# One exponential over two PSUM banks in a causal attention loop

## The chip, the cores and the metric

The kernel runs on all 8 NeuronCores of one Trainium2 chip, each core on its own sequence of 2048 tokens, with no traffic between cores. The metric is the device time of the slowest core in microseconds (us). The engines are named as in the profile: PE (TensorE, matmul), PEld (TensorE's weight load), DVE (VectorE), ACT (ScalarE), POOL (GpSimd) and SP (SyncE).

## The reference, cut to what matters

One pre-norm transformer layer: causal attention with 8 heads of width 128 over 2048 tokens, and then a mixture of experts with 8 experts and a shared one. The change is in the attention alone.

```python
x = x + attn(layernorm(x))
x = x + moe(layernorm(x))
# attn, for each batch entry b and head h
s = einsum('bihd,bjhd->bhij', q, k) / 128
s = s - 1e30 * (i < j)
p = softmax(s, axis=-1)
o = einsum('bhij,bjhd->bihd', p, v)
```

## The kernel before

The program writes out one instruction list for each engine. Every engine works through its list strictly in order and waits on semaphores. Each DVE, ACT and POOL instruction also waits for the one before it on its own engine. PSUM has eight banks of 128 x 512 F32, `ps[0]` to `ps[7]`. `bank_prod` emits a matmul that waits until the earlier readers of its bank are done (`bank.frees`), and `bank_cons` emits a reader that waits until the bank is written (`bank.ready`).

The work runs in this order: loading and transposing x, layernorm, then the heads, the output projection, a second layernorm, the router, and the nine experts. For each head h there are three stages in a row: `emit_passA(h)` (a bound on the scores, with squares on POOL), `emit_qkv_rope(h+1)` (projection and rotation for the next head) and `emit_passB(h)`, which holds the change.

`emit_passB` loops over four query chunks `qc` of 512 queries. A chunk has `nkt = 4*qc + 4` key tiles of 128 keys: 4, 8, 12 and 16, so 40 in a head and 320 on a core. For one key tile `kt` the steps are:

- S (L595): a matmul writes the scores, 128 keys x 512 queries, into bank 4 for an even `kt` and bank 5 for an odd one.
- mask (L601), for the last four key tiles of a chunk (the diagonal ones): DVE adds the mask to the bank in place.
- exp (L607): ACT writes exp(scores) as bf16 into one of the two halves of `pT`.
- O (L581) and L (L586): two matmuls that accumulate the output in bank 6 and the row sums in bank 7. They are always issued for the previous key tile, kept in `pend`.

So PE's list reads S0, S1, OL0, S2, OL1, S3, and so on: OL(k) stands behind S(k+1) and ahead of S(k+2). OL(k) waits for exp(k), and S(k+2) needs the bank that exp(k) read.

A chunk ends with the reciprocal of the row sums on DVE (L616), an F32 matmul that spreads it over the partitions through bank 5 (L620), its copy (L623) and the scaling of the output (L627). S0 of the next chunk follows L620 on PE at once. S1 waits for the copy L623, because it uses bank 5.

Of the kernel before, what the change touches and what calls it, by code (L numbers as in the profile page):

```python
# [7 lines left out]
F32 = mybir.dt.float32  # L8
BF16 = mybir.dt.bfloat16
AF = mybir.ActivationFunctionType  # L10
# [4 lines left out]
DM = 1024  # L15
NH = 8
DH = 128
# [100 lines left out]
def build_nc(dbg=False):  # L118
    nc = bass.Bass("TRN2", target_bir_lowering=False)
# [33 lines left out]
    big = nc.alloc_sbuf_tensor("big", [128, 32768], BF16)  # L153
# [1 line left out]
    csn = nc.alloc_sbuf_tensor("csn", [128, 4096], BF16)  # L155
    s_sb = nc.alloc_sbuf_tensor("s_sb", [128, 3072], F32)
    maskm = nc.alloc_sbuf_tensor("maskm", [128, 896], BF16)
    pT = nc.alloc_sbuf_tensor("pT", [128, 1024], BF16)
    identb = nc.alloc_sbuf_tensor("identb", [128, 128], BF16)
    identf = nc.alloc_sbuf_tensor("identf", [128, 128], F32)  # L160
    pmat_sb = nc.alloc_sbuf_tensor("pmat_sb", [128, 128], BF16)
    onesb = nc.alloc_sbuf_tensor("onesb", [128, 1], BF16)
    ones1 = nc.alloc_sbuf_tensor("ones1", [1, 128], F32)
    rwT = nc.alloc_sbuf_tensor("rwT", [128, KC * 8], BF16)
    rw_raw = nc.alloc_sbuf_tensor("rw_raw", [8, DM], BF16)
    bias_rep = nc.alloc_sbuf_tensor("bias_rep", [128, 8], F32)
    cwtok = nc.alloc_sbuf_tensor("cwtok", [128, 128], F32)
    lg_sb = nc.alloc_sbuf_tensor("lg_sb", [128, 128], F32)
# [14 lines left out]
    negmh = nc.alloc_sbuf_tensor("negmh", [128, 1], F32)  # L183
    mh_sb = nc.alloc_sbuf_tensor("mh_sb", [1, 8], F32)

    bigf = big[:, :].bitcast(F32)
    csnf = csn[:, :].bitcast(F32)
    sf = s_sb

    ps = [PsBank(nc.alloc_psum_tensor(f"ps{i}", [128, 512], F32).ap()) for i in range(8)]  # L190

    stack = ExitStack()
    mk = lambda name: Ch(stack.enter_context(nc.semaphore(name)))
# [15 lines left out]
    ac = mk("ac")  # L209
# [4 lines left out]
    b = Builder()  # L214
# [8 lines left out]
    def bank_prod(bank, fn, waits=(), last=True):  # L223
        w = list(waits) + bank.frees
        toks = b.emit("tensor", fn, waits=w, incs=[(pe, 1)] if last else ())
        bank.frees = []
        if last:
            bank.ready = toks[0]
            return toks[0]
        return None  # L230

    def bank_cons(bank, eng, fn, waits=(), ch=dv):
        w = list(waits) + ([bank.ready] if bank.ready else [])
        tok = b.emit(eng, fn, waits=w, incs=[(ch, 1)])[0]
        bank.frees.append(tok)
        return tok
# [3 lines left out]
    t_mask = dma(ld, "sync", maskm[:, :], d["c_mask"])  # L240
# [54 lines left out]
    for g4 in range(4):  # L295
# [5 lines left out]
        for ti in range(4):  # L301
            tt = g4 * 4 + ti
            for kc in range(KC):
# [5 lines left out]
                          waits=[tok_ld, t_identf])  # L309
                dstc = kc * T + tt * 128  # L310
                bank_cons(bank, "vector",
                          lambda e, o=x_sb[:, dstc:dstc + 128], i=pap: e.tensor_copy(o, i))
# [4 lines left out]
    for kc in range(KC):  # L317
# [4 lines left out]
                  waits=[t_rw, t_identb])  # L322
        bank_cons(bank, "vector",
                  lambda e, o=rwT[:, kc * 8:(kc + 1) * 8], i=pap: e.tensor_copy(o, i))
# [3 lines left out]
                                              start=True, stop=True),  # L328
              waits=[t_eb, t_ones1])
    bank_cons(bank, "vector",  # L330
              lambda e, o=bias_rep[:, :], i=pap: e.tensor_copy(o, i))
# [180 lines left out]
    rope_done = [None] * NH  # L512
# [51 lines left out]
    def emit_passB(h, t_negmh):  # L564
        par = h % 2
        half = h // 4
        hh = h % 4
        qs = q_slice(par)
        ks = k_slice(par)
        for qc in range(NTS):  # L570
            ob = ps[6]
            lb = ps[7]
            nkt = 4 * qc + 4
            pend = None

            def emit_ol(item, s1):
                tex_, vsl_, ptb_, kt_ = item
                bank_prod(ob,
                          lambda e, o=ob.ap[:, :], l=vsl_, r=ptb_,
                          s0=(kt_ == 0), s1_=s1:  # L580
                          e.matmul(o, l, r, start=s0, stop=s1_),  # L581
                          waits=[tex_, t_v_done[half]], last=s1)
                bank_prod(lb,
                          lambda e, o=lb.ap[0:1, :], r=ptb_,
                          s0=(kt_ == 0), s1_=s1:
                          e.matmul(o, onesb[:, :], r, start=s0, stop=s1_),  # L586
                          waits=[tex_], last=s1)

            for kt in range(nkt):
                sb_ = ps[4 + (kt % 2)]  # L590
                bank_prod(sb_,
                          lambda e, o=sb_.ap[:, :],
                          l=ks[:, kt * 128:(kt + 1) * 128],
                          r=qs[:, qc * 512:(qc + 1) * 512]:
                          e.matmul(o, l, r, start=True, stop=True),  # L595
                          waits=rope_done[h])
                if kt >= 4 * qc:
                    moff = 384 - 128 * (kt - 4 * qc)
                    tmk = bank_cons(sb_, "vector",
                                    lambda e, o=sb_.ap[:, :],  # L600
                                    m=maskm[:, moff:moff + 512]: e.tensor_add(o, o, m),  # L601
                                    waits=[t_mask])
                    sb_.ready = tmk
                ptb = pT[:, (kt % 2) * 512: (kt % 2) * 512 + 512]
                tex = bank_cons(sb_, "scalar",
                                lambda e, o=ptb, i=sb_.ap[:, :]:
                                e.activation(o, i, AF.Exp, bias=negmh[:, 0:1],  # L607
                                             scale=1.0 / DH),
                                waits=[t_negmh], ch=ac)
                vsl = big[:, kt * 512 + hh * 128: kt * 512 + hh * 128 + 128]  # L610
                if pend is not None:
                    emit_ol(pend, s1=False)
                pend = (tex, vsl, ptb, kt)
            emit_ol(pend, s1=True)
            til = bank_cons(lb, "vector",
                            lambda e, o=invl_row, i=lb.ap[0:1, :]: e.reciprocal(o, i))  # L616
            bank5 = ps[5]
            bank_prod(bank5,
                      lambda e, o=bank5.ap[:, :]:
                      e.matmul(o, ones1[:, :], invl_row, start=True, stop=True),  # L620
                      waits=[til])
            tsc = bank_cons(bank5, "vector",
                            lambda e, o=scale_rep, i=bank5.ap[:, :]: e.tensor_copy(o, i))  # L623
            ocol = o_col + h * T + qc * 512
            bank_cons(ob, "vector",
                      lambda e, o=big[:, ocol:ocol + 512], i=ob.ap[:, :]:
                      e.tensor_mul(o, i, scale_rep),  # L627
                      waits=[tsc])
        qk_free[par] = (pe, pe.n)
        pT_free[0] = (pe, pe.n)  # L630
# [3 lines left out]
    for h in range(NH):  # L634
        t_negmh = emit_passA(h)
# [14 lines left out]
    for mc in range(2):  # L650
        dwo = wo_slice(mc % 2).rearrange("p (c n) -> p c n", c=KC)
        t_wo_mc[mc] = dma(wd_wo[mc % 2], "gpsimd", dwo, wo_flat[:, :, mc * 128:(mc + 1) * 128],
                          waits=[qk_free[mc % 2]])
    for mc in range(KC):
        par = mc % 2
        for ts in range(NTS):
            bank = ps[(mc * NTS + ts) % 4]
            for c in range(KC):
                ocol2 = o_col + c * T + ts * 512
                bank_prod(bank,  # L660
                          lambda e, o=bank.ap[:, :],
                          l=wo_slice(par)[:, c * 128:(c + 1) * 128],
                          r=big[:, ocol2:ocol2 + 512],
                          s0=(c == 0), s1=(c == KC - 1):
                          e.matmul(o, l, r, start=s0, stop=s1),  # L665
                          waits=[t_wo_mc[mc], t_o_all], last=(c == KC - 1))
            xcol = mc * T + ts * 512
            bank_cons(bank, "vector",
                      lambda e, o=x_sb[:, xcol:xcol + 512], i=bank.ap[:, :]:
                      e.tensor_add(o, o, i),  # L670
                      waits=dbg_x0_tok)
        if mc + 2 < KC:
# [3 lines left out]
                                  waits=[(pe, pe.n)])  # L676
    t_x2 = (dv, dv.n)
    if dbg and "o" in dbg:
        dbg_gate_x2.append(dma(st, "sync", d["d_o"], big[:, 8192:24576],
                               waits=[t_o_all]))  # L680
# [7 lines left out]
    for tt in range(NTT):  # L688
        bank = ps[4 + tt % 2]
        for kc in range(KC):  # L690
            bank_prod(bank,
                      lambda e, o=bank.ap[:, 0:8],
                      l=xn_sb[:, kc * T + tt * 128: kc * T + (tt + 1) * 128],
                      r=rwT[:, kc * 8:(kc + 1) * 8],
                      s0=(kc == 0), s1=(kc == KC - 1):
                      e.matmul(o, l, r, start=s0, stop=s1),
                      waits=[xn_tok[tt // 4]], last=(kc == KC - 1))
        t_lg.append(bank_cons(bank, "vector",
                              lambda e, i=bank.ap[:, 0:8],
                              o=lg_sb[:, tt * 8:(tt + 1) * 8]:  # L700
# [7 lines left out]
    def m1bc(t):  # L708
# [3 lines left out]
           waits=t_lg, incs=[(dv, 1)])  # L712
# [3 lines left out]
           incs=[(dv, 1)])  # L716
    vnop()
    b.emit("vector", lambda e: e.tensor_max(m1a[:, :], kd128[:, 0:32:2], kd128[:, 1:32:2]),
           incs=[(dv, 1)])
    vnop()  # L720
    b.emit("vector", lambda e: e.tensor_sub(kd128[:, :], lg_sb[:, :], m1bc(m1a)),
           incs=[(dv, 1)])
# [3 lines left out]
           incs=[(dv, 1)])  # L726
    vnop()
    b.emit("vector", lambda e: e.tensor_scalar_mul(mska[:, :], km1a[:, :], -3e38),
           incs=[(dv, 1)])
    vnop()  # L730
    b.emit("vector", lambda e: e.tensor_add(mska[:, :], lg_sb[:, :], mska[:, :]),
           incs=[(dv, 1)])
# [3 lines left out]
           incs=[(dv, 1)])  # L736
# [3 lines left out]
           incs=[(dv, 1)])  # L740
    vnop()
    b.emit("vector", lambda e: e.tensor_max(m2a[:, :], kd128[:, 0:32:2], kd128[:, 1:32:2]),
           incs=[(dv, 1)])
    vnop()
    b.emit("vector", lambda e: e.tensor_sub(d12a[:, :], m1a[:, :], m2a[:, :]),
           incs=[(dv, 1)])
    vnop()
    b.emit("vector", lambda e: e.tensor_sub(kd128[:, :], lg_sb[:, :], m1bc(m2a)),
           incs=[(dv, 1)])
# [3 lines left out]
                 incs=[(dv, 1)])[0]  # L753
    tp1 = b.emit("scalar", lambda e: e.activation(p1a[:, :], d12a[:, :], AF.Sigmoid),
                 waits=[t_d], incs=[(ac, 1)])[0]
    tp2 = b.emit("scalar", lambda e: e.activation(p2a[:, :], d12a[:, :], AF.Sigmoid,
                                                  scale=-1.0),
                 incs=[(ac, 1)])[0]
# [3 lines left out]
           waits=[tp1], incs=[(dv, 1)])  # L762
# [3 lines left out]
           waits=[tp2], incs=[(dv, 1)])  # L766
    vnop()
    tcw = b.emit("vector", lambda e: e.tensor_add(cwtok[:, :], mska[:, :], kd128[:, :]),
                 incs=[(dv, 1)])[0]
    for tt in range(NTT):  # L770
# [3 lines left out]
                  lambda e, o=papt, i=cwtok[:, tt * 8:(tt + 1) * 8]:  # L774
                  e.transpose(o, i, identf[:, :]),
                  waits=[tcw])
        t_cw_rows.append(
            bank_cons(bankt, "vector",
                      lambda e, o=csnf[0:8, tt * 128:(tt + 1) * 128], i=papt:
# [4 lines left out]
    if dbg and "cw" in dbg:  # L784
        t_cw_rows = t_cw_rows + [dma(st, "sync", d["d_cw"], cwtok[:, :],
                                     waits=t_cw_rows)]
    if dbg and "lg" in dbg:
        t_cw_rows = t_cw_rows + [dma(st, "sync", d["d_lg"], lg_sb[:, :],
                                     waits=t_cw_rows)]
# [43 lines left out]
    for ei, e_ in enumerate(e_order):  # L833
# [3 lines left out]
        if not shared:  # L837
# [3 lines left out]
            else:  # L841
                tok_cp = dma(sw_cw, "sync", csnf[0:1, 0:2048], csnf[e_:e_ + 1, 0:2048],
                             waits=[(pe, pe.n)] + t_cw_rows)
                cwsrc = csnf[0:1, 0:2048]
                tok_cwsrc = [tok_cp]
            for tsb in range(NTS):
                bank = ps[tsb % 2]
                bank_prod(bank,
                          lambda e, o=bank.ap[:, :],
                          r=cwsrc[0:1, tsb * 512:(tsb + 1) * 512]:  # L850
# [180 lines left out]
```

How the kernel before makes its waits and increments, by code:

```python
        def run(e, ws=ws, fn=fn, rincs=rincs):  # L75
            for sem, v in ws:
                e.wait_ge(sem, v)
            inst = fn(e)
            for sem, amt in rincs:
                inst = inst.then_inc(sem, amt)
```

## Time and profile before

| | us |
|---|---|
| median of 3 runs (4823.49 to 4825.1) | 4824.67 |
| the profiled execution, its own time | 4822.22 |
| its span on the slowest core (core 2) | 4820.7 |
| spans of the eight cores | 4816.1 to 4820.7 |
| PE busy | 4021.4 (83%) |
| DVE busy | 1557.8 (32%) |
| ACT busy | 581.5 (12%) |
| the 320 exps of L607 | 219.9 in all, 0.687 each |

The profile is of one execution. Times in rows of the timeline are counted from the start of the span. A matmul row begins when the matmul starts; matmuls are pipelined and their ends are modelled, so the distance from start to start says what one costs. In square brackets a row has the idle time of its engine before it and what ended that. The mean granted TensorE clock over the span is 0.885 of full speed on every core; in single stretches it is either 0.50 (1.2 GHz) or 1.00 (2.4 GHz).

### The profile page before, as it was taken

To read this page: it belongs to the slowest core of one execution; us is meant where nothing else is said; L and a number is where in the kernel's file an instruction comes from. 1 tells how busy PE (TensorE), PEld (TensorE's weight loads), DVE (VectorE), ACT (ScalarE), POOL (GpSimd) and SP (SyncE) were. 2 spreads that over 40 slices of the span, in tenths; PEclk is the share of its full clock that TensorE was granted. 3 is DMA by queue.
4 is the path that set the end of the run, shared out by engine and by line. 5 is a ranking of instruction groups with operands and counts; after the bars stand their busy time and mean duration, and the time that the engine had idled before them with its cause. 6 is when DMAs were issued, how large, how long until landed. Compare 5 with 4: busy or idle time off the path is not lost.

```text
span 4820.7 us, 48101 instructions; the slowest of 8 cores (4816.1 to 4820.7 us)
## 1 busy us (share of the span) xinstructions
PE 4021.4 (83%) x16329; PEld 1672.1 (35%) x16650; DVE 1557.8 (32%) x2516; ACT 581.5 (12%) x933; POOL 668.8 (14%) x649
## 2 busy tenths in 40 slices
PE   5365566555574699999999999999999999999998
PEld 2021112111121244444444444444444444444443
DVE  4633333333336332232232232332322322322324
ACT  0002220112220010010010110110110110110100
POOL 0621101111104311011111110110110110111100
PEclk9576677676686699999999999999999999999996
DMA  4000000000010243343343334334333433434422
GB/s 99 0 9 5 5 5 5 5 0 5 3 11 5 27 40 37 34 40 37 35 40 38 36 37 39 35 36 40 35 37 35 40 36 36 40 35 40 39 28 79
DMA packets 480750, 143.01 MB, mean 30 GB/s; under 512 B 473738, under 2 KB 476154, under 8 KB 480514
## 3 DMA queue, kind: packets, MB, share of 16 engines
q0 software_dynamic: 475488, 122.72, 26.4%
q1 hardware_dynamic: 5026, 17.20, 1.0%
q8 instruction: 141, 2.31, 0.2%
q14 instruction: 95, 0.78, 0.1%
HBM read 254.15 MB, written 8.39 MB: 54 GB/s over the span
## 4 chain that ended last, share of the span: by engine, by line
PE 79%; DVE 11%; issue 4%; POOL 3%; ACT 2%; DMA 1%; DVEq 0%; ACTq 0%; POOLq 0%; SPq 0%
PE ps L871 21%; PE ps L932 21%; PE ps L884 20%; PE ps L480 3%; DVE s_sb L616 2%; PE ps L581 2%; PE ps L586 2%; PE ps L595 2%; PE ps L620 1%; DVE xn_sb L351 1%; ACT pT L607 1%; POOL pT L528 1%; PE ps L665 1%; PE ps L456 1%; POOL big L508 1%
## 5 line engine op out<-in xcount | busy, mean ns | idle before, releaser
L871 PE MATMUL ps<-xn_sb,w_sb 128*128 128x512 bf16 x4515 | 1054.3, 384 | 10.0 <-DVE s_sb L855 4.9
L884 PE MATMUL ps<-xn_sb,w_sb 128*128 128x512 bf16 x4515 | 1034.9, 379 | 4.9
L932 PE MATMUL ps<-big,w_sb 128*128 128x512 bf16 x4516 | 1003.9, 382 | 30.1 <-DVE big L906 25.1
L901 DVE TENSOR_TENSOR s_sb<-ps,s_sb 128x512 bf16<-128x512 f32 x512 | 354.2, 692 | 1178.5 <-PE ps L884 1102.8
L220 POOL DMA_DIRECT2D w_sb<-w x360 | 333.9, 931 | 2777.2 <-PE ps L884 1800.6
L892 ACT ACTIVATE s_sb<-ps 128x512 bf16<-128x512 f32 x576 | 344.0, 597 | 2636.6 <-PE ps L871 2422.5
L932 PEld LDWEIGHTS ps<-big,w_sb 128*128 128x128 bf16 x4608 | 454.1, 99 | 580.0 <-issue 46.6
L871 PEld LDWEIGHTS ps<-xn_sb,w_sb 128*128 128x128 bf16 x4608 | 454.7, 99 | 573.8 <-issue 43.0
L884 PEld LDWEIGHTS ps<-xn_sb,w_sb 128*128 128x128 bf16 x4608 | 450.9, 98 | 543.7
L941 DVE TENSOR_TENSOR x_sb<-x_sb,ps 128x512 f32<-128x512 f32 x288 | 198.0, 687 | 836.8 <-PE ps L932 792.1
L607 ACT ACTIVATE pT<-ps,negmh 128x512 bf16<-128x512 f32 x320 | 219.9, 687 | 682.8 <-DVE ps L601 414.4
L906 DVE TENSOR_TENSOR big<-s_sb 128x512 bf16<-128x512 bf16 x576 | 245.2, 426 | 63.0 <-DVE s_sb L901 3.7
L581 PE MATMUL ps<-pT,big 128*128 128x512 bf16 x315 | 144.3, 458 | 75.4 <-ACT pT L607 62.6
L601 DVE TENSOR_TENSOR ps<-ps,maskm 128x512 f32<-128x512 f32 x128 | 89.6, 700 | 278.1 <-PE ps L595 275.1
L595 PE MATMUL ps<-big 128*128 128x512 bf16 x307 | 147.5, 481 | 24.4 <-DVE s_sb L623 14.4
L620 PE MATMUL ps<-s_sb,ones 1*128 1x512 f32 x64 | 65.3, 1121 | 117.3 <-DVE s_sb L616 117.3
L528 POOL TENSOR_TENSOR pT<-big 128x512 bf16<-128x512 bf16 x64 | 66.4, 1038 | 596.7 <-PE ps L620 546.7
L586 PE MATMUL ps<-pT,onesb 128*1 128x512 bf16 x320 | 141.4, 442 | 4.9 <-DVE ps L601 3.5
L480 PE MATMUL ps<-xn_sb,w_sb 128*128 128x512 bf16 x498 | 139.1, 444 | 3.6 <-DVE big L460 1.6
L495 PE MATMUL ps<-s_sb,pmat_sb 128*128 128x512 bf16 x64 | 31.8, 497 | 122.3 <-DVE s_sb L491 122.3
L616 DVE RECIPROCAL s_sb<-ps 1x512 f32<-1x512 f32 x32 | 107.0, 3345 | 62.0 <-PE ps L586 62.0
L508 POOL TENSOR_TENSOR big<-s_sb 128x512 bf16<-128x512 f32 x64 | 80.7, 1261 | 293.1 <-DVE s_sb L504 293.1
(108 smaller groups left out, 1503.2 us busy)
## 6 DMA issues: line engine op xcount, KB each, us to landing
w_sb<-w POOLq DMA_DIRECT2D x288, 256.0 KB, 5.1
w_sb<-w POOLq DMA_DIRECT2D x72, 512.0 KB, 6.8
big<-x SPq DMA_DIRECT2D x4, 2048.0 KB, 15.7
out<-big SPq DMA_DIRECT2D x4, 2048.0 KB, 6.6
w_sb<-wv POOLq DMA_DIRECT2D x2, 1024.0 KB, 21.1
w_sb<-wq POOLq DMA_DIRECT2D x8, 256.0 KB, 6.0
w_sb<-wk POOLq DMA_DIRECT2D x8, 256.0 KB, 6.7
w_sb<-wo POOLq DMA_DIRECT2D x8, 256.0 KB, 4.5
```

What stands on the lines that cost most here:

```text
L220: return b.emit(eng, lambda e, o=out_ap, i=in_ap: e.dma_start(out=o, in_=i), waits=waits, incs=[(ch, 16)], nochain=True)[0]
L480: e.matmul(o, l, r, start=s0, stop=s1),
L581: e.matmul(o, l, r, start=s0, stop=s1_),
L586: e.matmul(o, onesb[:, :], r, start=s0, stop=s1_),
L595: e.matmul(o, l, r, start=True, stop=True),
L607: e.activation(o, i, AF.Exp, bias=negmh[:, 0:1], scale=1.0 / DH),
L871: e.matmul(o, l, r, start=s0, stop=s1),
L884: e.matmul(o, l, r, start=s0, stop=s1),
L892: lambda e, o=sb_b, i=gb_.ap[:, :]: e.activation(o, i, AF.Silu),
L901: e.tensor_mul(o, i, c),
L906: e.tensor_mul(o, a, bb),
L932: e.matmul(o, l, r, start=s0, stop=s1),
```

## The change

The key tiles are taken in pairs. Both S matmuls of a pair are issued, both masks where there are masks, and then one exp over banks 4 and 5 together: 128 x 1024 instead of two of 128 x 512. For that the eight PSUM banks become slices of one allocation, and `pT` doubles to two halves of 1024 columns. Both O/L pairs of matmuls wait for the one exp. `pend` still holds back one key tile, so the loop at the end of the pair issues OL of the odd tile of the previous pair and then OL of the even tile of this pair. PE's list now reads S0, S1, OL0, S2, S3, OL1, OL2, S4, S5, OL3, OL4, and so on.

`rw_raw`, the landing place of the router weights, moves from an own buffer into `big`, beyond the part in which x is staged. Its DMA stays where it was in POOL's list.

```diff
-    pT = nc.alloc_sbuf_tensor("pT", [128, 1024], BF16)
+    pT = nc.alloc_sbuf_tensor("pT", [128, 2048], BF16)
-    rw_raw = nc.alloc_sbuf_tensor("rw_raw", [8, DM], BF16)
+    rw_raw = big[0:8, 16384:16384 + DM]
-    ps = [PsBank(nc.alloc_psum_tensor(f"ps{i}", [128, 512], F32).ap()) for i in range(8)]
+    PS = nc.alloc_psum_tensor("psall", [128, 4096], F32)
+    ps = [PsBank(PS[:, i * 512:(i + 1) * 512]) for i in range(8)]
+    ps45 = PS[:, 2048:3072]
...
-            for kt in range(nkt):
-                sb_ = ps[4 + (kt % 2)]
-                bank_prod(sb_,
...
-                ptb = pT[:, (kt % 2) * 512: (kt % 2) * 512 + 512]
-                tex = bank_cons(sb_, "scalar",
-                                lambda e, o=ptb, i=sb_.ap[:, :]:
-                                e.activation(o, i, AF.Exp, bias=negmh[:, 0:1],
-                                             scale=1.0 / DH),
-                                waits=[t_negmh], ch=ac)
-                vsl = big[:, kt * 512 + hh * 128: kt * 512 + hh * 128 + 128]
-                if pend is not None:
-                    emit_ol(pend, s1=False)
-                pend = (tex, vsl, ptb, kt)
+            for kp in range(nkt // 2):
+                for ki in range(2):
+                    kt = 2 * kp + ki
+                    sb_ = ps[4 + ki]
+                    bank_prod(sb_,
...
+                ptb2 = pT[:, (kp % 2) * 1024: (kp % 2) * 1024 + 1024]
+                w = [t_negmh, ps[4].ready, ps[5].ready] + ps[4].frees + ps[5].frees
+                tex = b.emit("scalar",
+                             lambda e, o=ptb2: e.activation(o, ps45, AF.Exp,
+                                                            bias=negmh[:, 0:1],
+                                                            scale=1.0 / DH),
+                             waits=w, incs=[(ac, 1)])[0]
+                ps[4].frees.append(tex)
+                ps[5].frees.append(tex)
+                for ki in range(2):
+                    kt = 2 * kp + ki
+                    vsl = big[:, kt * 512 + hh * 128: kt * 512 + hh * 128 + 128]
+                    ptb = pT[:, (kp % 2) * 1024 + ki * 512: (kp % 2) * 1024 + ki * 512 + 512]
+                    if pend is not None:
+                        emit_ol(pend, s1=False)
+                    pend = (tex, vsl, ptb, kt)
```

## Rows read from the trace of the kernel before

**Rows 1.** The page, busy us (share of the span) and count of instructions.

```profile
PE 4021.4 (83%) x16329; PEld 1672.1 (35%) x16650; DVE 1557.8 (32%) x2516; ACT 581.5 (12%) x933; POOL 668.8 (14%) x649
```

**Rows 2.** Groups by line and shape on ACT: busy us, mean ns | idle before.

```profile
L892 ACT ACTIVATE s_sb<-ps 128x512 bf16<-128x512 f32 x576 | 344.0, 597 | 2636.6 <-PE ps L871 2422.5 <-remote 182.6 <-ACT s_sb L892 6.7
L607 ACT ACTIVATE pT<-ps,negmh 128x512 bf16<-128x512 f32 x320 | 219.9, 687 | 682.8 <-DVE ps L601 414.4 <-PE ps L595 230.1 <-PE ps L620 36.1
L389 ACT ACTIVATE s_sb<-s_sb 1x512 f32<-1x512 f32 x8 | 5.0, 628 | 269.6 <-DVE s_sb L387 269.6
...
L549 ACT ACTIVATE mh_sb<-mh_sb 1x1 f32<-1x1 f32 x8 | 1.6, 202 | 0.7
```

**Rows 3.** Timeline, head 2, third chunk: a diagonal pair, then the chunk's end.

```profile
686.45 0.39 PE L595 MATMUL ps<-big 128*128 128x512 bf16 x1
...
687.01 0.70 DVE L601 TENSOR_TENSOR ps<-ps,maskm 128x512 f32<-128x512 f32 x1 [8.47 <-PE ps L595]
...
687.86 0.69 ACT L607 ACTIVATE pT<-ps,negmh 128x512 bf16<-128x512 f32 x1 [1.24 <-DVE ps L601]
...
689.31 0.39 PE L595 MATMUL ps<-big 128*128 128x512 bf16 x1
...
692.49 0.38 PE L581 MATMUL ps<-pT,big 128*128 128x512 bf16 x1 [0.25 <-ACT pT L607]
...
693.35 3.35 DVE L616 RECIPROCAL s_sb<-ps 1x512 f32<-1x512 f32 x1 [1.84 <-PE ps L586]
```

**Rows 4.** Timeline, the same chunk: a pair without mask at full clock.

```profile
682.47 0.39 PE L595 MATMUL ps<-big 128*128 128x512 bf16 x1
...
683.01 0.69 ACT L607 ACTIVATE pT<-ps,negmh 128x512 bf16<-128x512 f32 x1 [0.37 <-PE ps L595]
...
683.84 0.38 PE L581 MATMUL ps<-pT,big 128*128 128x512 bf16 x1
...
684.46 0.39 PE L595 MATMUL ps<-big 128*128 128x512 bf16 x1
```

**Rows 5.** Timeline, the second chunk: a pair without mask at half clock.

```profile
660.59 0.61 PE L595 MATMUL ps<-big 128*128 128x512 bf16 x1
...
663.55 0.61 PE L595 MATMUL ps<-big 128*128 128x512 bf16 x1
```

**Rows 6.** Timeline, the third chunk's first pair, at half clock.

```profile
676.81 0.61 PE L595 MATMUL ps<-big 128*128 128x512 bf16 x1
...
677.89 0.59 PE L595 MATMUL ps<-big 128*128 128x512 bf16 x1 [0.47 <-DVE s_sb L623]
...
678.63 0.69 ACT L607 ACTIVATE pT<-ps,negmh 128x512 bf16<-128x512 f32 x1 [0.37 <-PE ps L595]
...
679.72 0.61 PE L595 MATMUL ps<-big 128*128 128x512 bf16 x1
```

**Rows 7.** Timeline, the first chunk: masks of its first pair, its second pair, its end.

```profile
644.30 1.50 DVE L601 TENSOR_TENSOR ps<-ps,maskm 128x512 f32<-128x512 f32 x2
...
647.00 0.61 PE L595 MATMUL ps<-big 128*128 128x512 bf16 x1
...
647.79 0.70 DVE L601 TENSOR_TENSOR ps<-ps,maskm 128x512 f32<-128x512 f32 x1 [1.99 <-PE ps L595]
...
650.95 0.58 PE L581 MATMUL ps<-pT,big 128*128 128x512 bf16 x1 [0.38 <-ACT pT L607]
...
652.22 3.35 DVE L616 RECIPROCAL s_sb<-ps 1x512 f32<-1x512 f32 x1 [2.25 <-PE ps L586]
```

**Rows 8.** Busy us (x) by stretch, head 2's third and fourth chunk; PEclk is the granted clock.

```profile
676.80:682.10 5.30, 4.62 (x10) 0.79 (x9) 1.38 (x2) 2.21 (x4) 0.00 (x0) 0.50 0.00 0
682.10:693.40 11.30, 8.87 (x28) 2.41 (x27) 2.85 (x5) 6.04 (x9) 0.00 (x0) 1.00 0.00 0
698.80:706.00 7.20, 5.98 (x13) 1.14 (x13) 1.38 (x2) 3.31 (x5) 0.00 (x0) 0.50 0.00 0
706.00:720.10 14.10, 11.29 (x36) 3.15 (x35) 2.86 (x5) 7.68 (x12) 0.00 (x0) 1.00 0.01 1
```

More of the change, by code:

```diff
@@ L587, in emit_ol @@
                           waits=[tex_], last=s1)
-            for kt in range(nkt):
-                sb_ = ps[4 + (kt % 2)]
-                bank_prod(sb_,
[L592 to L603, printed above, removed]
-                ptb = pT[:, (kt % 2) * 512: (kt % 2) * 512 + 512]
-                tex = bank_cons(sb_, "scalar",
-                                lambda e, o=ptb, i=sb_.ap[:, :]:
-                                e.activation(o, i, AF.Exp, bias=negmh[:, 0:1],
-                                             scale=1.0 / DH),
-                                waits=[t_negmh], ch=ac)
-                vsl = big[:, kt * 512 + hh * 128: kt * 512 + hh * 128 + 128]
-                if pend is not None:
-                    emit_ol(pend, s1=False)
-                pend = (tex, vsl, ptb, kt)
@@ new lines, in emit_passB @@
+            for kp in range(nkt // 2):
[3 more added lines that the diff above has]
+                    bank_prod(sb_,
+                              lambda e, o=sb_.ap[:, :],
+                              l=ks[:, kt * 128:(kt + 1) * 128],
+                              r=qs[:, qc * 512:(qc + 1) * 512]:
+                              e.matmul(o, l, r, start=True, stop=True),
+                              waits=rope_done[h])
+                    if kt >= 4 * qc:
+                        moff = 384 - 128 * (kt - 4 * qc)
+                        tmk = bank_cons(sb_, "vector",
+                                        lambda e, o=sb_.ap[:, :],
+                                        m=maskm[:, moff:moff + 512]: e.tensor_add(o, o, m),
+                                        waits=[t_mask])
+                        sb_.ready = tmk
+                ptb2 = pT[:, (kp % 2) * 1024: (kp % 2) * 1024 + 1024]
[14 more added lines that the diff above has]
+                    pend = (tex, vsl, ptb, kt)
```

## The prediction

> **What bounds the kernel now.** The page comes first: PE is busy for 83% of the span and ACT for 12% [rows 1]. That average is mostly the experts, which the change does not touch. So the groups by line on ACT come next. They say what the removed thing is worth where it stands: the 320 exps take 219.9 us, but ACT stood idle for 682.8 us ahead of them, 414.4 of it until a mask and 230.1 until a score matmul [rows 2]. ACT is starved in this stage, so its busy time is not what sets the stage's length. What does is read from the timeline of one head's pass B, in four pieces, together with the granted clock by stretch.
>
> In what follows a pair is the way from the S matmul of an even key tile to the S matmul of the next even tile. Before the change it is a closed chain, because S(k+2) stands behind OL(k) on PE and OL(k) waits for exp(k).
>
> - Without mask, at full clock, the chain is S start to exp start 0.54, exp 0.69, exp end to O start 0.14, and O and L together 0.62 until the next S. The sum is 1.99, and the two S starts are 1.99 apart [rows 4]. PE could issue the six matmuls in 6 x 0.31 = 1.86, so PE and the chain are nearly level.
> - Without mask at half clock PE itself is the bound: 2.96 for six matmuls, 0.49 each [rows 5].
> - Diagonal, at full clock, the mask comes in: S start to mask start 0.56, mask 0.70, 0.15, exp 0.69, 0.14, O and L 0.62. That is 2.86, and the S starts are 2.86 apart [rows 3].
>
> **The change part by part.** The order on PE matters most. Before, OL(k) had S(k+1) and OL(k-1) between it and its own S. In the new list the pair's exp can start only after both S matmuls (and both masks), and ahead of the waiting OL(2p) stands only OL(2p-1), two matmuls. Behind the waiting instruction on PE are L(2p) and both S matmuls of the next pair, and behind those on DVE and ACT the next masks and the next exp. So the longer exp, the second S and the second mask all enter the chain in series. Nothing covers them.
>
> *The length of the new exp, E.* No row shows a 1024-column one. From below: 128 x 512 without the pointer to a bias takes 597 ns and 1 x 1 takes 202, so 0.773 ns for each further element, and E is at least 687 + 512 x 0.773 = 1083 ns. The same step from 1 x 1 to 1 x 512 in one kind of operand gives (628 - 202) / 511 = 0.834, and E = 687 + 427 = 1114 ns. From above, two exps: 2 x 687 = 1374 ns, if crossing into the second bank cost a new start [rows 2]. I take 1.11 us, because the second pair of rows varies only the number of elements. The Trainium skill, page "ScalarE: Activation LUTs", section "What ACT_TABLE_LOAD costs", gives about 280 ns + 0.833 ns per element with a bias held in a pointer operand. By it the exp would be 1133 ns, and the sum below 160 x 0.02 = 3 us more.
>
> Each kind of pair is now chained again, with the same gaps:
>
> - *No mask, full clock:* second S 0.31 after the first (PE's pitch, half of the 0.62), then 0.54, 1.11, 0.14, 0.62 = 2.72 against 1.99 [rows 4]. That is +0.73.
> - *No mask, half clock:* second S 0.49 later, S to exp 0.74 [rows 6], 1.11, 0.14, O and L 2 x 0.49 = 3.46 against 2.96 [rows 5]. That is +0.50.
> - *First pair of a chunk, except in the first chunk:* S1 waits for L623 and starts 1.08 after S0; then 0.74, 1.11, 0.14, 0.98 = 4.05 against 2.91 [rows 6]. That is +1.14.
> - *Diagonal pair, full clock:* the second mask starts 0.80 after the first, since two of them take 1.50 with 0.70 each [rows 7]. Then 0.56 + 0.80 + 0.70 + 0.15 + 1.11 + 0.14 + 0.62 = 4.08 against 2.86 [rows 3]. That is +1.22.
> - *Last pair of a chunk, from its S to the reciprocal, full clock:* before, 693.35 - 689.31 = 4.04. After: 3.46 until the first O, 0.62 to the second O and 0.86 from there to the reciprocal = 4.94 [rows 3]. That is +0.90.
> - *The first chunk, at half clock:* its first pair before takes 2.70 from the first mask to the next S (647.00 - 644.30); after, 0.80 + 0.70 + 0.15 + 1.11 + 0.14 + 0.98 = 3.88, so +1.18. Its last pair before takes 5.22; after, 0.79 + 0.80 + 0.70 + 0.15 + 1.11 + 0.14 = 3.69 to the first O, 0.98 to the second, 1.27 to the reciprocal = 5.94, so +0.72 [rows 7].
>
> *Counting.* A head has 20 pairs: in the first chunk 2; in the others one first pair, 1, 3 and 5 middle pairs without mask, one diagonal and one last pair. The clock decides which price the middle ones have. In head 2 it is at 0.50 for the first 5.3 us of the third chunk and the first 7.2 us of the fourth, and at 1.00 for the rest, through diagonal stretches with gaps as well [rows 8]. That is the first pair and about one middle pair in each chunk at half clock. I keep that by pairs: 3 middle ones at half clock, 6 at full. A head then costs 1.18 + 0.72 + 3 x 1.14 + 3 x 0.50 + 6 x 0.73 + 3 x 1.22 + 3 x 0.90 = 17.6 us. Eight heads: 141 us.
>
> *The rest costs nothing.* The 160 exps saved shorten ACT's busy time by 160 x (1.374 - 1.114) = 42 us, but ACT waits here anyway, and after the change PE waits for a longer one instead. The PSUM slices are the same banks. `rw_raw` moves to columns that nothing else writes before the router weights are transposed; the DMA keeps its place, and its cover is the load of x. The larger `pT` adds no instruction. The stages around pass B depend on its last matmul and its last scaling only, so they start later by the same amount. The weight loads for the next head, issued on POOL at the start of pass B, only get more time. Should one of these cost something after all, it is a single transfer or a start of a few us, not 320 times something.
>
> The sum against the profiled execution is 4822.2 + 141 = 4963. The median is 2.5 us above that execution, so the forecast for it is 4966 us, 2.9% slower.
>
> **The rivals.**
>
> *The clock stays at half (13 in 100).* The new chain leaves gaps in PE's work in every pair: at half clock 2.96 of 3.46 us are matmuls, at full clock 1.86 of 2.72, and in diagonal pairs 1.86 of 4.08. If the clock then never rises in pass B, a head pays more on 6 middle pairs (3.46 - 2.72 = 0.74), 3 diagonal ones (0.79 + 0.80 + 0.70 + 0.15 + 1.11 + 0.14 + 0.98 = 4.67, against 4.08: 0.59) and 3 last ones (5.94 - 4.94 = 1.00): 9.2 us. The time becomes 4966 + 74 = 5040. For it speaks that the clock falls to 0.50 behind each chunk's reciprocal already. Against it speaks that the clock held 1.00 through diagonal stretches in which PE idled for about a third [rows 3, 8]. The Trainium skill, page "TensorE: Matmul & The Clock Gate", section "A second HAM failure mode: psum-queue depth-cycling", reports that small PE pauses between groups of matmuls, made by cycling through PSUM banks, let the clock swing between the levels. The rows just named do not show such a swing inside a chunk, only at its end.
>
> *The clock rises at the same time, not at the same pair.* As the pairs are longer, less of the list would lie before the rise. That takes about 0.6 us from each of three chunks, 14 us in all: 4952. I count it with the forecast.
>
> *Crossing the bank costs a start (10 in 100).* With E = 1.374 every one of the 160 pairs is 0.26 longer: 4966 + 42 = 5008.
>
> *The clock falls in part (8 in 100).* If it drops in the long waits of diagonal pairs alone, up to 3 x (0.59 + 1.00) x 8 = 38 us are added: up to 5004.
>
> *The waits are hidden (5 in 100, within 0.2%).* This would be so if both OLs of the previous pair stood behind the new S matmuls: four matmuls, 1.24 us, would then lie beside the exp. It needs an order on PE other than the one the list has; PE does no later matmul before one that waits.
>
> *ACT is what counts (2 in 100, faster).* If the stage were as long as ACT's list, the saving of 0.26 us for each pair would come back: 4825 - 42 = 4783. It decides only where ACT is busy back to back, which needs ACT's idle 682.8 us near nothing [rows 2]. To be faster by the chain, a pair without mask would need E under 1.99 - 0.31 - 0.54 - 0.14 - 0.62 = 0.38 us, less than the exp of 512 columns takes.
>
> **How the numbers follow.** The forecast case holds 62 in 100, with its own range of 4940 to 4985. Below, it is the 4952 of the earlier rise, 5 us less for E = 1.083, and 7 us for a second S that starts a little sooner than the 0.31 of an average matmul. Above, it is one more middle pair at half clock in three chunks of each head, 3 x 0.74 x 8 = 18 us. The range of 4935 to 5020 takes in the long exp and the part-time fall of the clock, and leaves out the clock that stays at half and the cases of no loss: 80 in 100. About 0.2% (10 us) is what a measurement of this kernel can tell from no change. Slower holds 0.93 (all cases but the last two), the same 0.04 and faster 0.03 (of the hidden waits 4 and 1 in 100, and the 2 of ACT).
>
> **What would show it right or wrong.** L607 should have 160 instructions of 128 x 1024 with a mean near 1114 ns; near 1374 would be the bank rival. PE's idle time ahead of L581, put down to L607, should be far longer than before. At full clock S matmuls of even tiles should be 2.7 us apart without mask and 4.1 with. From its first S to its reciprocal the third chunk should take 4.05 + 3.46 + 2 x 2.72 + 4.08 + 4.94 = 22.0 us, where it takes 16.5 now [rows 3, 6]. The stages outside pass B should keep their lengths. The prediction is wrong if PE's list in the trace shows four matmuls between the second S and the O that waits, or if the clock's rise comes much later than 5 to 7 us into a chunk.

## The result and the profile after

| | before | after |
|---|---|---|
| median, us | 4824.89 | 5031.92 |
| ratio | | 1.0443 (95% interval 1.041 to 1.0475) |
| profiled execution, us | 4822.22 | 5031.98 |
| span of the slowest core | 4820.7 | 5030.2 |
| mean granted TensorE clock | 0.885 | 0.842 |

The change costs 207 us. The forecast had the sign and the longer chain, but only 141 us; 5032 lies outside the range of 4935 to 5020. It lies next to the first rival (the clock stays at half, 5040), which had 13 in 100. In some executions the cores of one die run at a lower clock and take longer; the ratios here are those of executions without this, and for defer_pair and two_exps_late, whose medians it moves, the time given is the ratio times 4825.

Lines of the page of the changed kernel: the busy times, the granted clock in 40 slices, and two groups of pass B. Behind them stand the clock's line and the group of the O matmuls from the page of the kernel before.

```profile
PE 4118.9 (82%) x16329; PEld 1672.6 (33%) x16650; DVE 1557.5 (31%) x2516; ACT 539.6 (11%) x773; POOL 668.8 (13%) x649
...
PEclk9575556555555769999999999999999999999997
...
L583 PE MATMUL psall<-pT,big 128*128 128x512 bf16 x314 | 186.8, 595 | 179.8 <-ACT pT L611 179.8
L611 ACT ACTIVATE pT<-psall,negmh 128x1024 bf16<-128x1024 f32 x160 | 178.1, 1113 | 926.0 <-DVE psall L605 521.7
```

```profile
PEclk9576677676686699999999999999999999999996
...
L581 PE MATMUL ps<-pT,big 128*128 128x512 bf16 x315 | 144.3, 458 | 75.4 <-ACT pT L607 62.6
```

ACT has less to do, 539.6 us for 581.5 [rows 1], and is idle longer ahead of its exps, 926.0 us for 682.8 [rows 2]. An exp of 1024 columns takes 1113 ns. PE now waits 179.8 us for exps ahead of the O matmuls (L583), where it waited 62.6 us. In the clock's line (tenths of full speed, so half clock is 5), slices 4 to 13, where the heads run, show 5 and once 6; before, they showed 6 to 8.

The timeline of head 2, from the end of its first chunk through its second. "x2" is the two S matmuls of a pair, or its two masks.

```profile
707.26 3.35 DVE L626 RECIPROCAL s_sb<-psall 1x512 f32<-1x512 f32 x1 [3.73 <-PE psall L588]
...
712.72 0.61 PE L599 MATMUL psall<-big 128*128 128x512 bf16 x1
...
716.93 1.03 PE L599 MATMUL psall<-big 128*128 128x512 bf16 x2
...
718.12 1.11 ACT L611 ACTIVATE pT<-psall,negmh 128x1024 bf16<-128x1024 f32 x1 [2.46 <-PE psall L599]
...
719.38 0.58 PE L583 MATMUL psall<-pT,big 128*128 128x512 bf16 x1 [0.47 <-ACT pT L611]
...
720.41 1.03 PE L599 MATMUL psall<-big 128*128 128x512 bf16 x2
...
721.19 1.50 DVE L605 TENSOR_TENSOR psall<-psall,maskm 128x512 f32<-128x512 f32 x2 [6.74 <-PE psall L599]
...
722.84 1.11 ACT L611 ACTIVATE pT<-psall,negmh 128x1024 bf16<-128x1024 f32 x1 [3.61 <-DVE psall L605]
...
725.13 1.03 PE L599 MATMUL psall<-big 128*128 128x512 bf16 x2
...
728.83 0.59 PE L583 MATMUL psall<-pT,big 128*128 128x512 bf16 x1 [1.72 <-ACT pT L611]
...
731.16 3.35 DVE L626 RECIPROCAL s_sb<-psall 1x512 f32<-1x512 f32 x1 [3.74 <-PE psall L588]
```

The chain is the one that was forecast, link by link, at half clock: first pair 716.93 - 712.72 = 4.21 (forecast 4.05), pair without mask 3.48 (3.46), diagonal pair 725.13 - 720.41 = 4.72 (4.67), last pair 6.03 (5.94). What was not forecast is that the clock stays at half through the second and third chunk and almost to the end of the fourth. The busy times by stretch for this head's second, third and fourth chunk (the granted clock is the third number from the end):

```profile
712.70:731.20 18.50, 11.86 (x24) 2.20 (x24) 4.23 (x7) 4.45 (x4) 0.00 (x0) 0.50 0.01 1
736.60:762.00 25.40, 18.39 (x37) 3.29 (x36) 4.18 (x6) 6.68 (x6) 0.00 (x0) 0.50 0.00 0
767.50:799.00 31.50, 22.96 (x48) 4.32 (x48) 4.23 (x7) 8.91 (x8) 0.00 (x0) 0.55 0.00 0
```

Before, the same head's third and fourth chunk were at 1.00 after 5.3 and 7.2 us [rows 8].

The 32 reciprocals of a core give the length of every chunk: from one start to the next, less the 5.46 us between a reciprocal and the next chunk's first S (712.72 - 707.26). Means over the eight heads of the slowest core, in us, with the forecast sums beside them:

| chunk | before | forecast | half clock throughout | after |
|---|---|---|---|---|
| second | 13.0 | 4.05 + 3.46 + 4.08 + 4.94 = 16.5 | 18.1 | 18.2 |
| third | 16.9 | 22.0 | 4.05 + 3 x 3.46 + 4.67 + 5.94 = 25.0 | 25.2 |
| fourth | 21.0 | 27.4 | 32.0 | 32.1 |

The loss lies in pass B. On the slowest core the second to fourth chunks take 197 us more in all. The ways from a head's last reciprocal to the next head's first, with the first chunks in them, take 15 us more (forecast 8 x 1.90). From the last reciprocal to the end of the span it is 3421.1 us before and 3418.4 after.

### The profile page after: what moved, and what is told of

Same layout as the page of the kernel before. It is cut to its first block, busy times and chain, and to the rows that moved or that the text cites. A ratio compares the mean times of both kernels' runs of the same rounds, so it can differ in the third digit from the quotient of the medians.

```text
span 5030.2 us, 47621 instructions; the slowest of 8 cores (5019.8 to 5030.2 us)
## 1 busy us (share of the span) xinstructions
PE 4118.9 (82%) x16329; PEld 1672.6 (33%) x16650; DVE 1557.5 (31%) x2516; ACT 539.6 (11%) x773; POOL 668.8 (13%) x649
## 4 chain that ended last, share of the span: by engine, by line
PE 76%; DVE 11%; issue 4%; ACT 4%; POOL 3%; DMA 1%; DVEq 0%; ACTq 0%; POOLq 0%; another core or an unknown queue 0%; SPq 0%
PE psall L881 20%; PE psall L942 20%; PE psall L894 20%; ACT pT L611 4%; PE psall L482 2%; PE psall L599 2%; DVE s_sb L626 2%; PE psall L583 2%; PE psall L588 2%; DVE psall L605 2%; PE psall L630 1%; DVE xn_sb L353 1%; POOL pT L530 1%; PE psall L458 1%; PE psall L675 1%
## 5 line engine op out<-in xcount | busy, mean ns | idle before, releaser
L881 PE MATMUL psall<-xn_sb,w_sb 128*128 128x512 bf16 x4515 | 1051.6, 383 | 9.8 <-DVE s_sb L865 4.9
L894 PE MATMUL psall<-xn_sb,w_sb 128*128 128x512 bf16 x4515 | 1035.0, 379 | 4.8
L942 PE MATMUL psall<-big,w_sb 128*128 128x512 bf16 x4516 | 1003.1, 383 | 30.1 <-DVE big L916 25.2
L911 DVE TENSOR_TENSOR s_sb<-psall,s_sb 128x512 bf16<-128x512 f32 x512 | 354.2, 692 | 1175.4 <-PE psall L894 1100.2
L942 PEld LDWEIGHTS psall<-big,w_sb 128*128 128x128 bf16 x4608 | 453.6, 98 | 579.6 <-issue 45.2
L881 PEld LDWEIGHTS psall<-xn_sb,w_sb 128*128 128x128 bf16 x4608 | 453.6, 99 | 571.9 <-issue 39.2
L894 PEld LDWEIGHTS psall<-xn_sb,w_sb 128*128 128x128 bf16 x4608 | 450.4, 98 | 544.1
L902 ACT ACTIVATE s_sb<-psall 128x512 bf16<-128x512 f32 x576 | 343.9, 597 | 2635.5 <-PE psall L881 2421.6
L951 DVE TENSOR_TENSOR x_sb<-x_sb,psall 128x512 f32<-128x512 f32 x288 | 197.9, 687 | 836.0 <-PE psall L942 791.2
L583 PE MATMUL psall<-pT,big 128*128 128x512 bf16 x314 | 186.8, 595 | 179.8 <-ACT pT L611 179.8
L611 ACT ACTIVATE pT<-psall,negmh 128x1024 bf16<-128x1024 f32 x160 | 178.1, 1113 | 926.0 <-DVE psall L605 521.7
L588 PE MATMUL psall<-pT,onesb 128*1 128x512 bf16 x320 | 182.9, 571 | 11.7 <-ACT pT L611 11.4
L583 PEld LDWEIGHTS psall<-pT,big 128*128 128x128 bf16 x320 | 38.9, 122 | 312.0 <-issue 311.5
L482 PE MATMUL psall<-xn_sb,w_sb 128*128 128x512 bf16 x498 | 137.8, 441 | 3.6 <-DVE big L462 1.6
```

Of the source, the lines that this page charges most:

```text
L611: lambda e, o=ptb2: e.activation(o, ps45, AF.Exp, bias=negmh[:, 0:1], scale=1.0 / DH),
L902: lambda e, o=sb_b, i=gb_.ap[:, :]: e.activation(o, i, AF.Silu),
L911: e.tensor_mul(o, i, c),
```

## The experiments

All ran on 8 cores. Theories: A, the one exp waits for two scores and two masks with a single OL beside it, and the gaps this makes on PE also keep the clock down. B, the order on PE. C, the clock is low for a reason other than the gaps. D, the two-bank exp itself.

### two_exps: the order without the merge

```diff
-                tex = b.emit("scalar",
...
+                texs = []
+                for ki in range(2):
+                    sb_ = ps[4 + ki]
+                    ptb = pT[:, (kp % 2) * 1024 + ki * 512: (kp % 2) * 1024 + ki * 512 + 512]
+                    texs.append(bank_cons(sb_, "scalar",
...
-                    pend = (tex, vsl, ptb, kt)
+                    pend = (texs[ki], vsl, ptb, kt)
```

> The changed kernel with its order of matmuls on PE (S, S, OL of the odd tile before, OL of the even tile), but with two exps of 512 columns, and each O and L waiting for its own exp only. Theory A (the loss starts with the wait for one exp that needs both score matmuls and both masks): the chain of a pair is then again S to exp 0.54, 0.69, 0.14, O and L 0.62, so 1.99 us without mask and 2.86 with, as in the kernel before, and the time is 4825 us within 10, the mean clock 0.885. Rival B (the order on PE with a single OL as cover is the loss): 4950 us or more, clock about 0.845.

Measured: 4810.6 us, ratio 0.9969 (0.9958 to 0.9981), clock 0.885. B falls: the new order on PE costs nothing. It is even 15 us faster than the kernel before, more than the 10 us that I had allowed for. From its timeline, the last pair of head 2's first chunk and of its third:

```profile
643.57 1.03 PE L599 MATMUL psall<-big 128*128 128x512 bf16 x2
...
648.36 3.35 DVE L626 RECIPROCAL s_sb<-psall 1x512 f32<-1x512 f32 x1 [2.50 <-PE psall L588]
...
681.58 0.60 PE L599 MATMUL psall<-big 128*128 128x512 bf16 x2
...
684.44 0.60 PE L599 MATMUL psall<-big 128*128 128x512 bf16 x2
...
688.35 3.35 DVE L626 RECIPROCAL s_sb<-psall 1x512 f32<-1x512 f32 x1 [1.84 <-PE psall L588]
```

A diagonal pair takes 2.86, as before [rows 3]. The last pair takes 3.91 at full clock and 4.79 at half, against 4.04 [rows 3] and 5.22 [rows 7]. Its second S no longer stands behind an O that waits, so its mask and exp come earlier. That is 0.43 + 3 x 0.13 = 0.8 us a head, some 7 of the 15 us. Where the rest comes from was not looked for.

### two_exps_late: the wait without the merge

```diff
-                    pend = (texs[ki], vsl, ptb, kt)   # two_exps
+                    pend = (texs[1], vsl, ptb, kt)    # two_exps_late
```

> Two exps of 512 columns as in two_exps, but both OLs of a pair wait for the second one: the wait of the merged exp without the merge. The second exp ends 1.94 us after the first S at full clock where the merged one ends at 1.96, and at half clock the O starts 2.08 after the first S where the merged one lets it start at 2.48, so that PE has a gap of 0.12 instead of 0.5. Theory A: the wait itself costs 0.7 us a pair without mask at full clock, 0.8 a diagonal pair, 11.6 us a head, and the clock rises since the gaps at half clock are small: 4918 us within 25. Rival D (the two-bank exp is needed for the loss): 4811 us like two_exps.

Measured: ratio 1.0224 (1.0199 to 1.0248), 4933 us. The forecast was 4918 within 25. One changed wait costs 4933 - 4811 = 122 us, with exps of 512 columns as before; some of it comes through the clock, which is 0.874 to 0.879 where two_exps has 0.883 to 0.885. D falls as the main cause: the wait alone makes more than half of the loss.

### fill_all, fill_plain and fill_masked: the gaps and the clock

```diff
                     if pend is not None:
                         emit_ol(pend, s1=False)
+                    if ki == 0:
+                        filler(3 if kp >= 2 * qc else 1)   # fill_all
+                        filler(0 if kp >= 2 * qc else 1)   # fill_plain
+                        filler(3 if kp >= 2 * qc else 0)   # fill_masked
```

Each kernel is the changed one with one of the three lines; `filler(n)` issues n matmuls of 512 columns into bank 3, which nobody reads. The extra matmuls only add work.

> The changed kernel with extra matmuls of 512 columns into bank 3, which nobody reads, placed on PE right ahead of the O that waits for the exp: one in each pair without mask, three in each diagonal pair. At half clock the gap there is 0.47 us without mask and 1.72 with, and an extra matmul takes 0.49, so the chain itself gets at most 0.02 us longer in a pair. Theory A (the gaps that the merged exp leaves in each pair keep the granted clock at 0.50, and this is the difference between the 4966 forecast and the 5032 measured): the clock rises inside the chunks again, mean clock 0.88 or more, and the time falls to 4966 us within 20 in spite of the added work. Rival C (the clock is low for another reason, for instance the power drawn or the two-bank access): the clock stays at 0.84 and the time at 5032 to 5045 us.

Measured: 4954.73 us, ratio 1.0267 (1.0242 to 1.0292), clock 0.885. 288 extra matmuls make the changed kernel 77 us faster. Its third chunk in one head, in busy times by stretch and then in the timeline after the clock has risen:

```profile
715.10:720.10 5.00, 3.43 (x8) 0.71 (x8) 1.38 (x2) 1.11 (x1) 0.00 (x0) 0.50 0.00 0
720.10:737.00 16.90, 12.38 (x40) 3.01 (x38) 2.82 (x5) 5.57 (x5) 0.00 (x0) 0.93 0.00 1
```

```profile
722.66 0.60 PE L607 MATMUL psall<-big 128*128 128x512 bf16 x2
...
723.41 1.11 ACT L619 ACTIVATE pT<-psall,negmh 128x1024 bf16<-128x1024 f32 x1 [1.77 <-PE psall L607]
...
724.67 0.38 PE L583 MATMUL psall<-pT,big 128*128 128x512 bf16 x1 [0.57 <-ACT pT L619]
...
725.29 0.60 PE L607 MATMUL psall<-big 128*128 128x512 bf16 x2
...
727.92 0.61 PE L607 MATMUL psall<-big 128*128 128x512 bf16 x2
...
731.40 0.38 PE L583 MATMUL psall<-pT,big 128*128 128x512 bf16 x1 [1.60 <-ACT pT L619]
...
732.01 0.61 PE L607 MATMUL psall<-big 128*128 128x512 bf16 x2
...
736.98 3.35 DVE L636 RECIPROCAL s_sb<-psall 1x512 f32<-1x512 f32 x1 [2.89 <-PE psall L588]
```

Now the full-clock prices of the forecast can be read too: without mask 725.29 - 722.66 = 2.63 (forecast 2.72), diagonal 4.09 (4.08), last pair 4.97 (4.94). The chunks take 16.9, 22.2 and 27.3 us in the mean, against 16.5, 22.0 and 27.4 in the forecast. So with a clock that rises inside the chunks, as was assumed, the forecast of 4966 is met within 11 us. C falls. One thing stays open: the extra matmuls close the gaps and add work at the same time, and no run adds work without closing gaps.

> As the run with extra matmuls, but only the one in each pair without mask; the diagonal pairs keep their gaps. If the gaps of the pairs without mask decide the rise and a risen clock holds through the diagonal ones, the time is within 15 us of the run with all of them (4966 to 4980). If the diagonal gaps keep the clock down too, it lies near the middle, about 5000 us. If the gaps are not the cause, 5032 or more.

Measured: 4977.63 us, ratio 1.0316 (1.0296 to 1.0336), clock 0.870. Filling the pairs without mask takes off 54 of the 77 us. The time lies in the band of 4966 to 4980, but 23 us from fill_all and not within 15, so the diagonal gaps have a part: its second chunks, with one middle pair, still take 17.9 us in the mean.

> The complement of fill_plain: three extra matmuls in each diagonal pair of the changed kernel and none in the pairs without mask. fill_all took 77 us off and fill_plain 54. If the two kinds of gap act each in its own stretch, this one takes off the rest, 23 us: 5009 within 15, with a mean clock near 0.855. If the gaps of the pairs without mask alone decide, 5025 or more; if any filling is enough to raise the clock for a whole chunk, 4980 or less.

Measured: 4983.19 us, clock 0.868 to 0.876. The ratio is 1.0276 with a wide interval (1.018 to 1.0372), because the kernel before varied from 4824 to 4885 us beside it, so the time itself is used here. The expectation of 5009 was wrong, and 4983 is next to the 4980 of "any filling is enough": filling the diagonal pairs alone takes off 49 us, so the savings of the two kinds do not add up. The mean lengths of the second, third and fourth chunk are 16.9, 23.8 and 29.2 us here, 17.9, 22.6 and 28.3 in fill_plain and 16.9, 22.2 and 27.3 in fill_all: the diagonal gaps decide in the short second chunk, the others in the long ones. Busy times by stretch in one head: the third chunk in two parts, and the fourth.

```profile
721.30:738.70 17.40, 13.99 (x29) 2.65 (x29) 2.78 (x4) 4.75 (x5) 0.00 (x0) 0.50 0.00 0
738.70:745.50 6.80, 4.66 (x15) 1.03 (x13) 1.44 (x3) 1.94 (x2) 0.00 (x0) 0.89 0.01 2
750.90:777.80 26.90, 17.50 (x55) 4.31 (x54) 4.20 (x7) 8.91 (x8) 0.00 (x0) 0.88 0.00 0
```

In the third chunk the clock stays at half through the four pairs without mask and rises among the filled diagonal ones, as theory A has it. But in the fourth it rises within the unfilled pairs, at 757.1, 6 us into the chunk. This happens in four of eight heads, 6 to 10 us into the chunk (by the reciprocals, those four chunks take 26.9 to 27.7 us); in the other four it rises only among the filled diagonal pairs (30.9 to 31.5 us). The changed kernel has the same gaps there and stayed at half almost throughout; in head 2 it rose at 796, inside the last diagonal pair with its gap unfilled. So the gaps make the rise unlikely rather than forbid it; what decides it in a single chunk is open.

### defer_pair and four_banks_merged: covering the merged exp

```diff
+                for pp in pendl:
+                    emit_ol(pp, s1=False)
+                pendl = []
...
-                    if pend is not None:
-                        emit_ol(pend, s1=False)
-                    pend = (tex, vsl, ptb, kt)
+                    pendl.append((tex, vsl, ptb, kt))
...
+                bb = 4 if kp % 2 == 0 else 2    # four_banks_merged only
...
-                    sb_ = ps[4 + ki]
+                    sb_ = ps[bb + ki]           # four_banks_merged only
```

In four_banks_merged the exp reads the same two banks, `bb` and `bb + 1`.

> The changed kernel with its merged exp, but both OLs of a pair held back until after both S of the next pair, so that four matmuls lie beside the exp. Theory A: at half clock PE is fully busy without mask again (2.96 us a pair), so the clock rises as before; at full clock the next S waits for the exp, 0.31 + 0.54 + 1.11 + 0.14 = 2.10 against 1.99, a diagonal pair takes 3.46 against 2.86, the last pair of a chunk still 0.9 more. In all 6.6 us a head, so 4877 us within 20, clock 0.87 or more. Rival D (what costs is the two-bank exp itself, whatever is beside it): 5000 us or more.

Measured: ratio 1.0118 (1.0094 to 1.0142), 4882 us, clock 0.876 to 0.880. Two pairs of one chunk at full clock:

```profile
706.99 0.69 PE L600 MATMUL psall<-big 128*128 128x512 bf16 x2
...
709.09 0.59 PE L600 MATMUL psall<-big 128*128 128x512 bf16 x2 [0.26 <-ACT pT L612]
...
712.55 0.59 PE L600 MATMUL psall<-big 128*128 128x512 bf16 x2 [1.72 <-ACT pT L612]
```

2.10 and 3.46 us, exactly the chains that were worked out. With four matmuls beside the same exp, 150 of the 207 us are gone. In these rows PE still waits for the exp ahead of the next S, which needs the exp's banks.

> The merged exp with the OLs held back by a pair as in defer_pair, and the pairs' scores alternating between banks 4/5 and 2/3 (unused in pass B), so that the next S waits for no exp. Theory A: with the chain cut, PE is the bound without mask (1.86 us at full clock), the first pairs of the chunks overlap (0.8 us saved in each), the diagonal end is level with before: 4790 us within 25, the clock at 0.885. If instead the merged exp has a cost of its own, it stays above 4825.

Measured: 4800.13 us, ratio 0.9962 (0.9933 to 0.999), clock 0.887. With that chain cut, the merged exp stands in a kernel that is faster than the one before, by 25 us. D is out: the exp over two banks is no loss by itself.

### across_merged and across_single: a version that beats both

The chunks run into each other. The accumulators alternate, and the end of a chunk is issued in the next one.

```diff
+        acc = [(ps[6], ps[7]), (ps[0], ps[1])]
...
+            for pp in pendl:
+                emit_ol(pp)        # reciprocal right after a chunk's last OL
...
+            if qc > 0 and kp == 2:
+                finish(qc - 1)     # spreading matmul, copy, scaling
```

> As four_banks_merged, and the chunks run into each other: output and row sums alternate between banks 6/7 and 0/1, the reciprocal is taken at a chunk's end, and its spreading matmul and the scaling are issued after the third pair of the next chunk. The wait of 5.5 us for the reciprocal leaves PE's list in three of four chunks of a head, and the clock no longer falls there. Theory A: some 25 us a head less than before, 4600 to 4680 us, clock above 0.9. If DVE's 3.35 us reciprocal ahead of masks is in the way: nearer 4750.

Measured: 4605.69 us, ratio 0.9546 (0.9527 to 0.9565), clock 0.904. This is within what was expected.

> The same as across_merged with two exps of 512 columns, each O and L waiting for its own. It says whether the merged exp is worth something once nothing waits in its chain. Without mask both are bound by PE, so level there; with mask the first O of a pair can start 1.2 us earlier. I expect it 5 to 30 us faster than across_merged. If the fixed part of each exp counted, it would be slower.

Measured: 4567.9 us, ratio 0.9467 (0.9449 to 0.9486), clock 0.907. Two exps of 512 columns beat the merged one by 38 us, more than the 5 to 30 expected. The O matmuls in the span from 300 to 1650 us, first in across_merged, then in across_single, and the busy times of one head's pass B in across_single:

```profile
L584 PE MATMUL psall<-pT,big 128*128 128x512 bf16 x314 | 132.6, 422 | 45.1 <-ACT pT L634 44.5
...
L584 PE MATMUL psall<-pT,big 128*128 128x512 bf16 x314 | 124.5, 396 | 18.8 <-ACT pT L636 14.3
```

```profile
368.00:411.00 43.00, 39.14 (x123) 10.26 (x125) 25.55 (x27) 27.48 (x40) 3.00 (x3) 0.95 0.14 13
```

From a head's first reciprocal to its last it takes 37.0 us where the kernel before took 67.3, in the mean of eight heads, and the clock holds near full through pass B. ACT is busy for 27.48 of the 43 us. So even here the fixed part of each exp, which the merge saves, is not what counts. PE waits 30 us less for exps ahead of the O matmuls than in across_merged, which fits an O that can start on its own, earlier exp; where the other 8 us come from is open.

## Why the prediction was wrong

1. *ACT is starved, so fewer exps save nothing.* Right: ACT's busy time fell by 42 us and its wait ahead of the exps rose.
2. *E = 1.11 us.* Right: 1113 ns. The second bank costs no new start; 1374 is out, and with it that rival. The formula of the Trainium skill, page "ScalarE: Activation LUTs", section "What ACT_TABLE_LOAD costs", gives 1133: its 0.833 ns per element agrees with (1113 - 687) / 512 = 0.832 here, and its fixed part is 20 ns more than measured.
3. *The second S, the second mask and the longer exp enter the chain in series.* Right, at both clocks: 3.48, 4.72 and 6.03 at half; 2.63, 4.09 and 4.97 at full in fill_all. Only the 2.72 without mask was 0.09 too long: from the first S to the exp it is 723.41 - 722.66 = 0.75 at full clock, where 0.31 + 0.54 = 0.85 was taken. two_exps_late shows that the wait alone makes more than half of the loss, and defer_pair that cover takes most of it away.
4. *Counting: "I keep that by pairs: 3 middle ones at half clock, 6 at full."* This step failed. The clock's rise was carried over from a list in which PE had no gap in the pairs at half clock [rows 5] to one with 0.47 us in each and 1.72 us in each diagonal one. The rows that spoke against the rival showed the clock holding at 1.00 through gaps [rows 3, 8]; they did not show it rising through them. In place of the assumed rise, head 2 was at 0.50 through its second and third chunk, and at 0.55 in the mean of its fourth. With the pairs priced right, 9.2 us a head moved from the rival to the result: 4966 + 74 = 5040 for no rise at all, and 5032 measured, with a few rises among the eight heads. fill_all, which brings the rise back by other means, is 77 us faster than the changed kernel.
5. *The price of the rival was right, its chance was too low.* 13 in 100 rested on rows that could not exclude it, as step 4 says. The Trainium skill, page "TensorE: Matmul & The Clock Gate", section "A second HAM failure mode: psum-queue depth-cycling", spoke for it, and was set aside because the rows of before showed no swing inside a chunk. The runs agree with it in part: small gaps do cost clock here, but what they show is a clock that stays at 0.50 for whole chunks and not one that swings between the levels.
6. *The rest costs nothing.* Right as far as it shows: with the same PSUM slices, `pT` and `rw_raw`, two_exps is faster than before, and the stages behind the heads kept their length.

## What to carry to other kernels

Before two instructions are merged, ask what waits for the first of them alone, and what lies beside the merged one on the engine that waits: here the merge put a second score and a second mask ahead of the first output matmul, and the 42 us it saved were on an engine that sat idle. When gaps are added to TensorE's work, price every matmul behind them at half clock as well as at full, and let a rise of the clock count only if the new list also has the dense stretch in which it rose. Where PSUM banks are free, more scores in flight and accumulators that alternate were worth far more (219 us with the merged exp, 257 with two) than the form of the exp, 38 us.

## What the runs showed of the hardware

- One ACT instruction over two adjacent PSUM banks, 128 x 1024, takes 1113 ns where 128 x 512 takes 687: 0.83 ns for each further column, nothing for the crossing.
- In head 2 of the changed kernel the granted clock stayed at 0.50 through the second and third chunk, 49 us from 712.7 to 762, while PE's work had a gap of 0.47 us in each pair without mask (1.5 in a chunk's first pair) and 1.72 in each diagonal pair. With one more matmul in the first kind and three in the second (fill_all) it rose at 722.4, some 7 us into the chunk that is shown. In single chunks it rose through unfilled gaps too: four of eight fourth chunks of fill_masked.
- Once risen, it held at 1.00 through diagonal pairs with 1.60 us of PE waiting behind the extra matmuls (fill_all, 723 to 739), and fell at 739.5, in the 3.7 us in which PE had nothing and DVE computed the reciprocal.
